# A denominator's product moved to GpSimd, ahead of the normalisation in its row

## The reference

```python
x = _layernorm(x, ln_g, ln_b)
last_x = jnp.pad(x[:, :-1], ((0, 0), (1, 0), (0, 0)))
k = (x * time_mix_k + last_x * (1.0 - time_mix_k)) @ Wk.T
v = (x * time_mix_v + last_x * (1.0 - time_mix_v)) @ Wv.T
r = (x * time_mix_r + last_x * (1.0 - time_mix_r)) @ Wr.T
td = jnp.exp(time_decay)
...
    den = den * td + kt          # kt is exp(k) of this token
    num = num * td + kt * vt
    return ((num, den), num / (den + 1e-08))
...
out = jax.nn.sigmoid(r) * wkv @ Wo.T
```

## Time and profile before

| | us |
|---|---|
| median of three runs | 1807.21 |
| lowest and highest run | 1803.85, 1813.75 |
| the profiled execution | 1808.79 |
| its span, first to last instruction | 1807.0 |
| PE, DVE, POOL, ACT busy | 1473.8, 1345.3, 1074.7, 1023.4 |
| the rwkv layer's reciprocals, first to last start | 358.9 to 512.0 |

### The profile page before, as it was taken

The page is one execution under the profiler, slowest core; times in us unless marked ns, Lnnn a source line. Parts: engine busy times, 40 slices in busy tenths (PEclk is TensorE's granted clock), DMA queues, the critical chain, the costliest instruction groups (busy, mean ns, idle before and its releaser), DMA issues. The chain is left out here.

```text
span 1807.0 us, 39131 instructions
## 1 busy us (share of the span) xinstructions
PE 1473.8 (82%) x10452; PEld 1354.6 (75%) x10452; DVE 1345.3 (74%) x3991; ACT 1023.4 (57%) x2541; POOL 1074.7 (59%) x1700
## 2 busy tenths in 40 slices
PE   8799999588849999997029999386999984079996
PEld 8699999477737999997019999385888873069996
DVE  7789998599987888886547777644787745447775
ACT  4688888233317888873026766224777721047764
POOL 7438886667733454533665666601789946646665
PEclk9899999699968999996569999656899956579998
DMA  5111100380001110002112221302222101122220
GB/s 187 54 37 31 35 29 7 85 204 1 1 13 49 36 36 31 30 1 93 59 56 58 65 63 44 94 8 73 83 78 84 63 1 41 46 61 65 64 54 11
DMA packets 93268, 96.23 MB, mean 53 GB/s; under 512 B 12072, under 2 KB 75709, under 8 KB 92576
## 3 DMA queue, kind: packets, MB, share of 16 engines
q1 hardware_dynamic: 83168, 76.70, 14.7%
q0 software_dynamic: 9920, 17.35, 2.9%
HBM read 63.75 MB, written 33.78 MB: 54 GB/s over the span
## 5 line engine op out<-in xcount | busy, mean ns | idle before, releaser
L1398 DVE TENSOR_TENSOR choice_hlo<-choice_h,choice_hhi 128x512 fp32r<-128x512 f32 x256 | 177.7, 735 | 22.7 <-ACT choice_hhi L1251 22.0
L1243 ACT ACTIVATE choice_h<-banks 128x512 f32<-128x512 f32 x256 | 152.6, 600 | 59.9 <-PE banks L1143 50.2
L791 DVE SCALAR_TENSOR_TENSOR top_h<-top_silu,top_xs,banks 128x176 f32<-128x176 f32 x364 | 128.5, 394 | 56.1 <-ACT top_silu L635 54.2
L840 POOL DMA_INDIRECT rt_rows<-X,top_slot x128 | 128.6, 1005 | 53.5 <-issue 38.1
L635 ACT ACTIVATE top_silu<-banks,top_xs 128x352 f32<-128x352 f32 x182 | 101.1, 555 | 88.0 <-PE banks L559 83.7
L1141 PE MATMUL banks<-choice_xin_hi,ec_w_hi 128*128 128x256 f32 x512 | 145.9, 285 | 4.8 <-ACT choice_xin_lo L1236 3.6
L1154 PE MATMUL banks<-choice_hhi,ec_w_hi 128*128 128x256 f32 x512 | 145.8, 285 | 2.6 <-DVE choice_hlo L1398 2.0
L1251 ACT ACTIVATE choice_hhi<-choice_h 128x512 fp32r<-128x512 f32 x256 | 146.5, 625 | 0.0
L1142 PE MATMUL banks<-choice_xin_lo,ec_w_hi 128*128 128x256 f32 x512 | 143.9, 281 | 0.0
L1143 PE MATMUL banks<-choice_xin_hi,ec_w_lo 128*128 128x256 f32 x512 | 143.9, 281 | 0.0
L1155 PE MATMUL banks<-choice_hlo,ec_w_hi 128*128 128x256 f32 x512 | 142.6, 279 | 0.0
(11 more groups left out here) (309 smaller groups left out, 5388.3 us busy)
## 6 DMA issues: line engine op xcount, KB each, us to landing
choice_token_row<-choice_tokens SPq DMA_DIRECT2D x64, 256.0 KB, 3.2
mlstm_run_row<-mlstm_run SPq DMA_DIRECT2D x32, 512.0 KB, 3.6
rt_rows<-rt_blank SPq DMA_DIRECT2D x2, 6188.0 KB, 35.9
top_xs<-rt_rows SPq DMA_DIRECT2D x182, 68.0 KB, 1.8
X<-in_x SPq DMA_DIRECT2D x8, 512.0 KB, 6.9
ec_stage<-in_ec_w SPq DMA_DIRECT2D x2, 2048.0 KB
X<-rt_y SPq DMA_DIRECT2D x8, 512.0 KB, 7.0
rt_rows<-X,top_slot POOLq DMA_INDIRECT x128
```

Of the source, the lines that this page charges most:

```text
L1243: act.activation(self.h[:, c, :], self.ph[c][:, :], ACT.Gelu).then_inc(self.gelu_done, 1)
L1398: dve.tensor_tensor(flat(self.hlo), self.h[:, c, :], flat(self.hhi).bitcast(F32), ALU.subtract).then_inc(self.hlo_done, 1)
```

## The change

In each batch the product for the denominator moves from VectorE to GpSimd, which first adds 1e-8 to `den` in place and then multiplies by `er1`; the sum `er1` moves from GpSimd to ScalarE, as an Identity with a bias of one, right behind `er`; and in GpSimd's step the denominator's two instructions stand ahead of the normalisation, where the sum stood behind it. VectorE's denominator scan now announces itself by a semaphore (`den_steps`), and the reciprocal waits for GpSimd.

```diff
@@ Rwkv.scalar, exps
             act.activation(self.er[:, u, :], self.pr[u][:, 0:T], ACT.Exp, scale=-1.0).then_inc(self.er_done, 1)
+            act.wait_ge(self.er_done, b + 1)
+            need(act, self.under_done, b - 1)
+            act.activation(self.er1[:, u, :], self.er[:, u, :], ACT.Identity, bias=self.one[:, :]).then_inc(self.er1_done, 1)
@@ Rwkv.vector, mix
-            dve.tensor_tensor_scan(self.den[:, u, :], td, self.ek[:, u, :], 0.0, ALU.mult, ALU.add)
+            need(dve, self.under_done, b - 1)
+            dve.tensor_tensor_scan(self.den[:, u, :], td, self.ek[:, u, :], 0.0, ALU.mult, ALU.add).then_inc(self.den_steps, 1)
             dve.wait_ge(self.ekv_done, b + 1)
             dve.tensor_tensor_scan(self.num[:, u, :], td, self.ekv[:, u, :], 0.0, ALU.mult, ALU.add).then_inc(self.scans_done, 1)
             if inside(b - 1):
                 update(b - 1, 1 - u)
-            dve.wait_ge(self.scans_done, b + 1)
-            dve.wait_ge(self.er1_done, b + 1)
-
-            dve.scalar_tensor_tensor(out=self.under[:, u, :], in0=self.den[:, u, :], scalar=1e-8, in1=self.er1[:, u, :],
-                                     op0=ALU.add, op1=ALU.mult).then_inc(self.under_done, 1)
             last(sh.moments.stats_of)
             dve.wait_ge(self.under_done, b + 1)
             dve.reciprocal(self.over[:, u, :], self.under[:, u, :]).then_inc(self.over_done, 1)
             last(sh.moments.gather_of)
             dve.wait_ge(self.over_done, b + 1)
+            dve.wait_ge(self.scans_done, b + 1)
@@ Rwkv.vector, before the loop
+        i = dve.memset(self.one[:, :], 1.0)
         i.then_inc(self.setup, 1)
@@ Rwkv.gpsimd
-        def er1(b, u):
-            apart(pool, self.under_done, b - 1, self.sh.passed)
-            apart(pool, self.er_done, b + 1, self.sh.passed)
-            pool.tensor_scalar(self.er1[:, u, :], self.er[:, u, :], 1.0, 1.0, ALU.mult, ALU.add).then_inc(self.er1_done, 1)
+        def under(b, u):
+
+            apart(pool, self.den_steps, 2 * b + 1, self.sh.passed)
+            den = self.den[:, u, :]
+            pool.tensor_scalar(den, den, 1.0, 1e-8, ALU.mult, ALU.add).then_inc(self.den_steps, 1)
+            apart(pool, self.over_done, b - 1, self.sh.passed)
+            apart(pool, self.er1_done, b + 1, self.sh.passed)
+            apart(pool, self.den_steps, 2 * b + 2, self.sh.passed)
+            pool.tensor_tensor(self.under[:, u, :], den, self.er1[:, u, :], ALU.mult).then_inc(self.under_done, 1)
...
         def step(s, u):
+            if inside(s):
+                under(s, u)
             if inside(s + 2):
                 norm(s + 2, u)
-            if inside(s):
-                er1(s, u)
             self.scale_next(pool, s - 2, u)
```

More of the change, by code:

```diff
@@ L1584, in __init__ @@
         self.rest = f("one_minus_mix", [P, 3])
-        self.td = f("decay_exp", [P, 1])
+        self.td, self.one = f("decay_exp", [P, 1]), f("one", [P, 1])
         self.w = f("w", [P, 4, C])
@@ L1598, in __init__ @@
         self.xT_ready, self.x1_done, self.kv_done, self.r_done = s("xT_ready"), s("x1_done"), s("kv_done"), s("r_done")
+        self.den_steps = s("den_steps")
         self.ek_done, self.er_done, self.er1_done = s("ek_done"), s("er_done"), s("er1_done")
```

## The result

The changed kernel takes 1868.45 us, median of four runs (1862.31 to 1869.9); the kernel before, measured with it, 1805.53 (1801.4 to 1813.75). The ratio is 1.0327, with a 95% interval of 1.0293 to 1.0362: 63 us slower, where +69 us (1876) was forecast. The profiled execution is the fastest of the four, 1862.31 us with a span of 1860.5. On another chip, where the kernel before took 1791.6 us, the changed one took 1853.84: ratio 1.0341 (1.0321 to 1.0361). Where traces of different chips can be compared, the difference lies mostly in the two top-2 layers: 304.3 and 300.2 us in the trace of the kernel before, 296.2 and 293.4 us in a trace on the other chip.

What follows compares the result with a forecast made beforehand. VectorE's row set the pace at 4.94 us a batch; the change makes a 6.92 us chain across engines. 1808.8 + 59.4 + 9.7 (TensorE's clock) = 1877.9, or 1876 us beside the median; range 1854 to 1910.

Steps and rivals of the forecast that it cites:

- The mechanism: Rwkv layer: normalisation of s+2 queues behind GpSimd's denominator work, delaying transposes and the projection of s+1; 6.92 us a batch.
- The terms of the chain: Steps from one denominator scan's start to the next, across GpSimd, TensorE, ScalarE and VectorE, summing to 6.92 us.
- GpSimd's product: Denominator times er1 on GpSimd, priced at 0.61 us like L319 or L321; 0.84 by the page's factor.
- GpSimd beside the scans: GpSimd's tensor_scalar beside the rest of VectorE's numerator scan: taken as 0.60 us, between 0.41 alone and 0.88 beside two scans.
- VectorE's gain: Losing the product (L1717) saves VectorE 0.06 us a batch, not 0.43, since it covered the statistics' wait for X's update.
- One sign of the list: In the changed profile VectorE would idle some tenths of a us ahead of the reciprocal, released by GpSimd's product.
- ScalarE's part: The new Identity right after er takes 0.38 to 0.57 us, taken at nothing; 0.4 us a batch if its cover went.
- TensorE's clock: TensorE's idle 2.7 us a batch may drop its clock to 1.2 GHz: 5 of 30 batches, 9.7 us in all.
- The last ring: The layer's last batch has no normalisation ahead of it and keeps 4.94 us.
- The low clock holds: Rival: more than half of the chain's batches run with TensorE at 1.2 GHz, 1897 to 1924 us; chance 0.13.
- Blocked by the scans: Rival: VectorE's scans block GpSimd's steps, 7.34 us a batch at full clock, 1889 us with the clock term; chance 0.12.
- not slower: Rival: the projection doesn't hang on the late tile, so the ring is 4.83 us, under VectorE's 4.88; 1805 us; chance 0.05.

Runs made afterwards that it cites:

- the sum's experiment: Kernel before with only the sum er1 moved from GpSimd to ScalarE, the product staying on VectorE: 1805.45 us, ratio 0.9972; again on another chip 1788.15 us, ratio 0.9984.
- the filled kernel: Changed kernel with five unread matmuls more in each of TensorE's steps, behind the scores: 1847.0 us, ratio 1.0334; again 1848.51 us, ratio 1.0321.
- the two others: Changed kernel without GpSimd's addition of 1e-8: 1889.74 us, ratio 1.0421; kernel before with GpSimd's old sum ahead of the normalisation: 1860.25 us, ratio 1.0291.

## Why the prediction was right, point by point

**The mechanism** was right: the chain through GpSimd's row, TensorE's transposes and the projection. Taking the order back removes all but 1.7 of the layer's 61.3 us, doing the order alone on other work brings it (28 us at full clock), and cutting it at TensorE's row removes it too.

**The terms of the chain**, expected against the rows of the ring above: to GpSimd's start 0.87, measured 0.88; the addition with its own wait 0.60 + 0.25 = 0.85, measured 434.16 - 433.39 = 0.77; the product 0.61, measured 0.72 long and 0.68 to the next start; normalisation 1.46, measured 1.47; TensorE's waking 0.19, measured 0.06; transposes 0.25, measured 0.27; projection 1.93, measured 2.01; ek to scan 0.76, measured 0.76. Sum 6.92, measured 6.90, in rings of 6.75 where the first steps are written out and 6.82 to 6.90 in the loop. The closeness of the sum is partly luck: TensorE's waking was too long by 0.13 and the addition by 0.08, the product too short by 0.07 and the projection by 0.08.

**GpSimd's product.** It took 0.72 us against VectorE's 0.41, whose instruction did the addition as well, so 1.8 times. By the factor of two of the Trainium skill's GPSIMD Engine Reference ("4.1 Engine selection") it would have been 0.84, an estimate. L319, the row that I priced it by, is 0.61, but its second input is one number per token spread over 128 columns, where the product has two full ones. The truth lay in the middle; that the spread input is what made the priced row shorter is likely and not shown.

**GpSimd beside the scans.** The numerator's scan ran beside the addition:

```profile
433.11 0.66 DVE L1716 TENSOR_TENSOR_SCAN rwkv_num<-rwkv_decay_exp,rwkv_ekv 128x256 f32<-128x256 f32 x1
```

The addition took 0.59 us, 0.18 more than the 0.41 of the sum alone and close to the middle value that I took. It is 0.59 in all 32 batches, always beside this scan, so no run has it alone. The rule of the Trainium skill's SBUF — State Buffer ("SBUF: two separate sides") that the loser blocks until the other's instruction is over would have had it start with the end of the numerator's scan at 433.11 + 0.66 = 433.77 and end at 434.18, and the product begin behind that; it began at 434.16. For this pair of instructions the rule's time is not what was seen. What the rows do show of the two engines beside each other is in the sum's experiment: 0.16 us of VectorE's scan were gone with GpSimd's sum.

**VectorE's gain.** The prediction had it as 0.06 us of 0.43, from the row at the layer's end. In the loop it is 0.01 at most: the statistics start 0.74 us after the update, as before:

```profile
433.69 0.39 DVE L1731 TENSOR_TENSOR X<-X,banks 128x256 f32 x1
...
434.43 0.49 DVE L262 BATCH_NORM_STATS2 bnstats<-X 128x6 f32 x2 [0.34 <-DVE X L1731]
...
434.92 1.75 DVE L1721 RECIPROCAL rwkv_over<-rwkv_under 128x256 f32<-128x256 f32 x1
```

The step was right and the term a little too large. One sign of the list did not come: the reciprocal was to wait some tenths for GpSimd's product. The product ends at 434.88 and the statistics at 434.92, and the reciprocal starts at 434.92; the profile has such a wait once in 32 batches, 1.3 us in the first.

**ScalarE's part.** The Identity took 0.51 us, within 0.38 to 0.57, and was over at 433.54, 0.62 us before the product started. Taken at nothing, it cost nothing but 0.3 us in the first batch, where the product waited for it; with the addition gone it became a link of the chain.

**TensorE's clock.** Forecast 5 rings of 30 at the low level, 9.7 us. In the profiled execution there were 3 long rings, 1.4, 1.2 and 1.7 us longer than their neighbours, 4.3 us together; against the filled kernel it is 3.3 and 3.7 us in two traces, and 1 us more in each without the longer last ring of the filled one. Of the 6 us between +69 and +63 us, 5.4 are this term. Three rows of TensorE from the two long rings in the middle of the layer:

```profile
498.44 0.60 PE L1639 MATMUL banks<-rwkv_x,rwkv_w_now 128*128 128x256 f32 x2
...
501.66 1.06 PE L1640 MATMUL banks<-rwkv_x,rwkv_w_before 128*128 128x256 f32 x2
...
506.23 0.64 PE L1630 MATMUL banks<-ident,rwkv_xn 128*128 128x128 f32 x2 [2.35 <-POOL rwkv_xn L321]
```

The matmuls took 0.60 up to 499.3 and 1.06 from 499.95 on, and are back at 0.60 at 509.9. A ring with its whole projection at the low clock, 8.85 us by the forecast, did not occur: each long ring was at 1.2 GHz only in part.

**The last ring** was taken as 4.94 and was 4.87; **the other layers** were taken as unmoved, and the medians agree with that as far as they can.

**The rivals.** "The low clock holds" did not come in this kernel, but it came close by: in the kernel without the addition, with a ring of 6.4 us instead of 6.9, more than half of the rings were long, and it cost 39 us in the layer. Its chance of 0.13 was not too high, but the reason given for it doesn't hold: I argued from the length of the pause, 2.7 us. The pause in the changed kernel is 2.8 us, in the two others 1.9 and 2.2 to 2.4, and it was the ones with the shorter pauses in which the clock fell often. So that only 3 rings of 31 were long is luck as far as the argument goes. What decides there is open; no run here separates the length of the pause from the length of the ring. "Blocked by the scans" and "not slower" did not come.

## What to carry to other kernels

An engine's row is a queue: before moving work ahead of something in it, ask who waits for what is now behind, and follow that round to where the moved work gets its own input; if the way closes within one iteration, the iteration is as long as the whole way, though every engine is idle a third of it. A busy engine gains nothing from losing an instruction that stood between a result and its reader: look at what the next instruction waits for. And once an iteration has pauses on TensorE, a shorter chain can be slower by the clock; compare rings at full clock first, and the total after.

## What the runs showed of the hardware

- TensorE's granted clock made an order of kernels that the work doesn't have. Rings of 5.9 and 6.4 us at full clock had means of 6.72 and 7.70; 3 and 4 unread matmuls a batch brought them to 5.9 and 6.45. The ring of 6.9 us, with the longest pause of the three, lost only 4 to 5 us in 214.
- One and the same VectorE instruction, the numerator's scan, took 0.66 us alone and 0.82 beside GpSimd's sum and small step; GpSimd's tensor_scalar took 0.41 alone and 0.88 beside two scans (the sum), and 0.59 beside the last half of one (the addition to the denominator).
- The Identity that adds a pointer bias to 256 columns in SBUF took 0.51 us on ScalarE, the exponential from PSUM 0.38.
- The layers that no experiment touched moved by up to 9 us each from one profiled execution to the next (mLSTM 341.5 and 350.8 us on one chip), and kernels whose rwkv layers agree within 1 us had medians 0.4% apart. Below some 10 us only the trace of the layer itself tells what an edit did.
